# Attention scores as two 64-row tiles in half steps, a new order of the TensorE slot, and one copy that frees a bank

## The reference

```python
# block 1, attention: 16 heads of 16
zn = (z - mu) / sqrt(var + EPS) * ln_scale + ln_bias
q, k, v = heads of zn @ w_qkv
att = softmax(q @ k.T / sqrt(16))            # 1024 x 1024 for each of 4 x 16 heads
block1 = z + (att @ v) @ w_proj + b_proj
# block 2: a gated shared network for all rows, and for 512 routed rows
# one of 8 experts, the two mixed by a softmax of two gate scores
```

## Time and profile before

| | before |
|---|---|
| median of 3 runs | 1079.07 us |
| the profiled execution, its own time | 1083.07 us |
| its span, first to last instruction | 1081.3 us |
| TensorE busy | 981.1 us (91%) |
| VectorE busy | 868.7 us (80%) |
| ScalarE busy | 600.4 us (56%) |
| GpSimd busy | 249.0 us (23%) |
| mean granted TensorE clock | 0.955 |

### The profile page before, as it was taken

One profiled execution on the slowest core, in us unless ns is written; L12 is line 12 of the kernel. 1 busy time (PEld: TensorE's weight loads), 2 busy tenths in 40 slices (PEclk: granted clock), 3 DMA queues, 4 the chain that ended last, 5 costly groups with the idle time before them and its releaser, 6 DMA issues.

```text
span 1081.3 us, 14462 instructions
## 1 busy us (share of the span) xinstructions
PE 981.1 (91%) x5348; PEld 389.9 (36%) x5348; DVE 868.7 (80%) x1762; ACT 600.4 (56%) x699; POOL 249.0 (23%) x297
## 2 busy tenths in 40 slices
PE   4279999999999999999999999999999999829983
PEld 3122332323343344333342343333423432317762
DVE  5288888899988989998889899989899896165655
ACT  3025677677765675667757756677467566600010
POOL 4060001101614220146321312433032024320102
PEclk9597999999999999999999999999999999957996
DMA  9905100510350204111601032016110001410001
GB/s 171 131 1 67 53 25 16 79 41 1 67 92 5 75 12 59 49 40 40 93 26 40 1 44 67 9 40 114 43 40 2 1 1 29 167 59 0 1 1 58
DMA packets 46518, 50.27 MB, mean 46 GB/s; under 512 B 8416, under 2 KB 39408, under 8 KB 46064
## 3 DMA queue, kind: packets, MB, share of 16 engines
q1 hardware_dynamic: 45104, 47.51, 20.9%
q10 hardware_dynamic: 960, 0.79, 0.7%
q0 software_dynamic: 384, 1.05, 0.3%
HBM read 13.94 MB, written 8.91 MB: 21 GB/s over the span
## 4 chain that ended last, share of the span: by engine, by line
PE 72%; DVE 21%; ACT 2%; DMA 2%; issue 2%; POOL 1%; SPq 0%; ACTq 0%; POOLq 0%; DVEq 0%
PE sc L832 20%; PE obank L846 16%; PE ring L818 13%; DVE mx L1052 13%; PE ring L739 9%; PE ring L761 5%; PE sc L922 4%; PE ring L731 3%; DVE st L987 2%; PE ring L872 2%; ACT prob L666 1%; DMA kp<-parts 1%; DVE hid L1009 1%; PE ring L866 1%; DMA x_sb<-x 0%
## 5 line engine op out<-in xcount | busy, mean ns | idle before, releaser
L1052 DVE TENSOR_REDUCE mx<-ring 128x1 f32<-128x512 f32 x1024 | 649.9, 684 | 82.2 <-PE ring L818 74.4
L666 ACT ACTIVATE prob<-sc 128x1024 f32<-128x1024 f32 x512 | 501.0, 1022 | 269.2 <-PE sc L832 269.1
L846 PE MATMUL obank<-prob,vaug 128*32 128x512 f32 x2048 | 273.3, 606 | 0.7 <-ACT prob L666 0.7
L832 PE MATMUL sc<-qp,kp 112*128 112x512 bf16 x1024 | 267.7, 383 | 1.5 <-DMA qp<-mp 0.7
L818 PE MATMUL ring<-kp,qp 48*128 48x512 bf16 x1024 | 224.8, 391 | 34.1 <-issue 20.0
L818 PEld LDWEIGHTS ring<-kp,qp 48*128 48x128 bf16 x1024 | 57.5, 93 | 360.9 <-DVE mx L1052 189.4
L832 PEld LDWEIGHTS sc<-qp,kp 112*128 112x128 bf16 x1024 | 83.8, 98 | 115.4 <-issue 38.7
L501 POOL TENSOR_SCALAR parts<-resid 128x1024 bf16<-128x1024 f32 x14 | 14.7, 1051 | 328.9 <-DVE resid L1042 328.6
L846 PEld LDWEIGHTS obank<-prob,vaug 128*32 128x32 f32 x2048 | 40.3, 108 | 61.9 <-issue 52.4
L731 PE MATMUL ring<-ident,zn 128*128 128x128 f32 x128 | 21.8, 310 | 31.9 <-DVE zn L1003 19.9
L739 PE MATMUL ring<-w,yT 128*128 128x256 f32 x192 | 48.6, 395 | 1.8 <-ACT yT L592 1.8
(11 more groups left out here) (178 smaller groups left out, 785.3 us busy)
## 6 DMA issues: line engine op xcount, KB each, us to landing
kp<-parts SPq DMA_DIRECT2D x96, 128.0 KB, 5.0
qp<-parts SPq DMA_DIRECT2D x180, 64.0 KB, 2.6
x_sb<-x SPq DMA_DIRECT2D x7, 1024.0 KB, 5.9
x_scratch<-x SPq DMA_DIRECT2D x4, 1024.0 KB, 4.4
out<-hid SPq DMA_DIRECT2D x4, 1024.0 KB, 4.6
kp<-ew SPq DMA_DIRECT2D x1, 2048.0 KB, 7.8
x_sb<-x SPq DMA_DIRECT2D x2, 512.0 KB, 4.6
qp<-mp SPq DMA_DIRECT2D x64, 4.0 KB, 1.7
```

The source lines that it names most:

```text
L666: nc.scalar.activation(prob[:, e % 2, 2 * a:2 * a + 2, :].rearrange("p g n -> p (g n)"), sbuf2[a][:, :], ACT.Exp, scale=0.25).then_inc(s_f ...
L832: ins = nc.tensor.matmul(dst[:, j * HALF:(j + 1) * HALF], kp[0:KM, h, kt * P:(kt + 1) * P], qp[0:KM, qh, h, :], start=True, stop=True)
L846: ins = nc.tensor.matmul(obank[i * VW:(i + 1) * VW, :], vaug[:, b % 2, kt, c0:c0 + VW], prob[:, v % 2, i, :], start=(kt == 0), stop=(kt == ...
L1052: nc.vector.tensor_reduce(mx[:, u % 2, n:n + 1], src[:, :], AX.X, ALU.max).then_inc(rv_free, 1)
```

## The change: what it does

In a slot TensorE now does the ring items first, then six pairs of matmuls and the value product. A pair is one matmul on rows 0 to 63 and one on rows 64 to 111. A score buffer is filled in two half steps: the first writes the largest products of both heads (`start=True`), the second adds the small ones (`stop=True`). The second half step waits on a new semaphore `s_largest` until the first is complete. ScalarE does all ring items of a slot before its exponentials. For `qk`, the fp32 copy alone frees the bank, and the bf16 copy is made from it in SBUF after a wait for it. Those who waited for the bf16 copy by `ra_free` now wait on `s_part`.

```diff
@@ ScalarE, ring_item of "qk" and the slot
-                    nc.scalar.activation(qkf[:, half], src[:, :], ACT.Copy).then_inc(s_part, 1)
-                    nc.scalar.activation(parts[:, c % 2, 0, half], src[:, :], ACT.Copy).then_inc(ra_free, 1)
+                    nc.scalar.activation(qkf[:, half], src[:, :], ACT.Copy).then_inc(ra_free, 1)
+                    sc.wait_ge(ra_free, TAKEN[key][1] + 1)
+                    nc.scalar.activation(parts[:, c % 2, 0, half], qkf[:, half], ACT.Copy).then_inc(s_part, 1)
...
-                items = [key for key in RING_AT[t] if key[0] in BY_ACT]
+                for key in RING_AT[t]:
+                    if key[0] in BY_ACT:
+                        ring_item(key)
                 for a in range(2):
...
-                    for key in items:
-                        if (key[0] in ("qk", "v")) == (a == 1):
-                            ring_item(key)
@@ residual, on VectorE (on GpSimd the same)
-                ve.wait_ge(ra_free, TAKEN["qk", b, c, 1][1] + 1)
+                ve.wait_ge(s_part, 2 * n + 2)
@@ TensorE
-                def scores(a):
+                def scores(a, largest):
...
-                    for j in range(2):
-                        h = g * GH + 2 * a + j
-                        ins = nc.tensor.matmul(dst[:, j * HALF:(j + 1) * HALF], kp[0:KM, h, kt * P:(kt + 1) * P],
-                                               qp[0:KM, qh, h, :], start=True, stop=True)
-                    ins.then_inc(s_full, 1)
+                    if largest:
+                        dst = open_s(2 * e + a)
+                    else:
+                        dst = sbuf2[a]
+                        pe.wait_ge(s_largest, 2 * e + a + 1)
+                    for low in range(2):
+                        j = low if largest else 1 - low
+                        h, rows = g * GH + 2 * a + j, slice(64 * low, 64 + KR * low)
+                        ins = nc.tensor.matmul(dst[:, j * HALF:(j + 1) * HALF], kp[rows, h, kt * P:(kt + 1) * P],
+                                               qp[rows, qh, h, :], start=largest, stop=not largest)
+                    ins.then_inc(s_largest if largest else s_full, 1)
...
-                if 0 <= e < NS:
-                    scores(0)
-                    scores(1)
                 for key in RING_AT[t]:
                     if key[0] not in ("max", "mt", "ot"):
                         ring_item(key)
+                if 0 <= e < NS:
+                    scores(0, True)
                 if t < NS:
                     max_products(range(0, 2))
+                if 0 <= e < NS:
+                    scores(1, True)
+                    scores(0, False)
+                    scores(1, False)
+                if t < NS:
+                    max_products(range(2, 4))
                 if 0 <= e - 1 < NS:
                     value_product(e - 1)
-                if t < NS:
-                    max_products(range(2, 4))
```

More of the change, by code:

```diff
@@ L231, in build @@
         s_free = sem("score_buffer_taken")
+        s_largest = sem("largest_products_summed")
         r_full = sem("ring_filled")
@@ L357, in _ @@
                 if part == 0:
-                    sp.wait_ge(ra_free, TAKEN["qk", 0, 0, 1][1] + 1)
+                    sp.wait_ge(s_part, 2)
                 elif part == 1:
@@ L492, in residual @@
                 n = 2 * KD * b + c
-                pool.wait_ge(ra_free, TAKEN["qk", b, c, 1][1] + 1)
+                pool.wait_ge(s_part, 2 * n + 2)
                 pool.wait_ge(s_third, n)
@@ L646, in _ @@
                 if part == 0:
-                    sc.wait_ge(ra_free, TAKEN["qk", 0, 1, 1][1] + 1)
+                    sc.wait_ge(s_part, 4)
                 elif part == 1:
@@ L820, in max_products @@
                                          start=True, stop=True).then_inc(r_full, 1)
-                def scores(a):
+                def scores(a, largest):
                     u, kt = e // 8, e % 8
                     g, qh = u % HU // NH, u % NH
-                    dst = open_s(2 * e + a)
                     if e == 0 and a == 0:
                         pe.wait_ge(s_fixed, 32)
-                    if kt == 0 and a == 0:
+                    if kt == 0 and a == 0 and largest:
                         pe.wait_ge(s_mrow[u % 2], 32 * (u // 2 + 1))
-                    for j in range(2):
-                        h = g * GH + 2 * a + j
-                        ins = nc.tensor.matmul(dst[:, j * HALF:(j + 1) * HALF], kp[0:KM, h, kt * P:(kt + 1) * P],
-                                               qp[0:KM, qh, h, :], start=True, stop=True)
-                    ins.then_inc(s_full, 1)
+                    if largest:
[9 more added lines that the diff above has]
+                    ins.then_inc(s_largest if largest else s_full, 1)
                 def value_product(v):
```

## The result

The changed kernel takes 1112.61 us (median of 4 runs, 1111.58 to 1113.86) against 1079.43 for the kernel before (4 runs beside it): ratio 1.030, 95% interval 1.028 to 1.033. It is slower by 33 us, where 29 were forecast. The profiled execution took 1112.55 us, its span is 1110.7, 29.4 above that of before.

A forecast was written before the change was run, and what follows sets the result against it. The prediction took TensorE to bound the kernel, VectorE 0.2 behind. Slots 27.9, last steps 6.9, absorbed -6 and prologue 0.3 gave +29.1: 1112 profiled, 1108 us on the median (2.7% slower), range 1095 to 1132.

The forecast's parts named there:

- the last steps: Steps after the last max product (e = 244 to 255): from 1.96 to 2.69 each, 6.9 us slower in all.
- TensorE bounds a plain slot, by 0.2 over VectorE: In a slot without a ring item (2.61 us) TensorE never pauses; VectorE's four maxima need 2.40.
- Modes: six pairs, 2.42: TensorE's work in a slot without a ring item: six pairs at 0.22, 0.10 and 1.00, 0.2 less than now.
- The ring's chain: Fourth max product waits for the first one's bank, 1.18 after its start; slots without ring items go from 2.61 to 2.71.
- The exponentials' chain: Buffer 1's next first half step waits for its exponential: 2.69 a step, hidden by 0.02 beside max products.
- Slots with ring items: Each item adds its stream, as before, and one more mode change, 0.10: from +0.03 (`ot`) to +0.19 (`qk`) a slot.
- What absorbs some: Slots already held by other waits, and those just behind them, feel the added wait less: -6 us, bounds 0 and 12.
- The last 4 us: Step from the profiled execution, forecast at 1112, to the median, taken as 4.0 below it: 1108 us.
- ScalarE's edits: `qk` bank freed 0.59 earlier: gain of 0 to 0.5 in the first slots; copies in the prologue +0.3; moved waits nothing.
- the rival at 1133: Pairs cost more than they stream: half steps 0.32 apart, +25, 1133 us; chance 0.15, of which 0.12 near 1120 to 1133.
- The rival on the fast side: The bank wait does not bind: slots without ring items at 2.42 to 2.45, about 1057 us; chance 0.05.

## Why the prediction was right

The direction was right, and so was the mechanism, with one weight misplaced. The size was near, 33 for 29; that the profiled execution came out within 0.3 us of its sum, and the last steps to the 0.1, is luck, as errors met in both.

- *TensorE bounds a plain slot, by 0.2 over VectorE.* Plain slots held 2.61 with shorter maxima. But elsewhere VectorE bounded more than I saw: 37 us went with half of its maxima's columns.
- *Modes: six pairs, 2.42.* 2.44 with both chains cut. The saving of 0.2 a slot is real and was never collected.
- *The ring's chain, 2.71.* M3 1.16 to 1.17 after M0 where I had 1.18, 0.24 (plain) to 0.27 (`qk`) after M2 where I had 0.30, VectorE 0.22 idle where I had 0.3; 2.70 with exponentials cut.
- *The exponentials' chain, 2.69, "hidden by 0.02".* Here lay the error of weight. It is 2.70, a tie with the ring's: cutting either one left plain slots at 2.70. By the half steps in the old order it suffices for the whole loss in plain slots. I presented the ring as the cause and this as a second chain that matters in the last steps; in plain slots it is as much the cause. The last steps cost 6.9, to the 0.1, but not by my reckoning. In the kernel before twelve of them, from value product to value product, took 25.8 us, 2.15 each, and not the 1.96 that I read out of the earlier trace rows: ScalarE wasn't all that held them. They take 31.6 now, +5.8. The other 1.1 belongs to where I count from, as M0 of slot 255 now stands 1.57 ahead of its slot's value product and not 0.32.
- *Slots with ring items.* Measured from the traces as medians, M0 to M0, each distance put down to the item of the second slot or the `mt` or `ot` of the first: `qk` +0.29 where I had +0.19; `z`, `a`, `x` +0.21 against +0.15; `p`, `h` +0.22 and `w` +0.19 against +0.11; `mt` +0.07 against +0.08; `ot` +0.07 against +0.03. The term that failed is the item's stream, which I took over from the kernel before, where the item stands behind scores in the same mode. Behind a change of mode its first pass costs more. A `qk` item takes 1.92 from its start to the next L0 behind the value product (18 times, with 0.53 from its first pass to its second and 0.43 between the others). Behind an `mt`, which is in full mode like the item, it takes 1.81 in the same kernel (6 times), as it did behind whole scores before:

```profile
371.92 0.28 PE L877 MATMUL ring<-ident,nm 128*16 128x128 f32 x1
372.03 1.88 PE L762 MATMUL ring<-zT,wk 128*128 128x512 f32 x4
373.85 0.39 PE L840 MATMUL sc<-qp,kp 64*128 64x512 bf16 x2
```

In the kernel with half steps alone it stands behind the half steps and takes 1.92 as well, so it is the change of mode and not the value product. That its weights are then no longer loaded behind a running matmul is argued from this, not shown.
- *What absorbs some, -6.* The sum from M0 of slot 12 to that of slot 255 came out at 27.9, my sum without this term, where with it I had 21.9. But the differences of medians, kind by kind and times the counts, add up to 33.4: the slots were undercounted by 5.5, most of it in those with items, and 5.5 was absorbed. So the 6 stands, and it is the items' term that was too small. The 2.6 before slot 12 and the 2.7 after the last value product no term had.
- *The last 4 us.* For the profiled execution I had +29.1, to 1112; it took 1112.55, its span +29.4 (27.9 + 6.9 - 2.6 - 2.7). Slots and last steps cost 34.8 where I had 28.8, and the 5.3 that came off outside them hid this. The median came out 4.6 above my 1108, since I had taken the profiled execution's 4.0 above the median along, while that of the changed kernel stands on its median. The lower clock of before's profiled execution behind the last value product, told above, fits that, and so does the medians' difference of 33.2, near the 34.8.
- *ScalarE's edits, nothing.* 1.0004. I had M2 as "late by some 0.2 with both copies"; it was late by 0.12 and covered.
- *The rivals.* Pairs stand 0.22 apart, so the rival at 1133 falls. The Trainium skill (TensorE: Matmul & The Clock Gate, Part 3: Packing small matmuls) gives 3.07 for four row tiles, from which I had estimated 0.28 a pair; with two tiles, here, no such loss is to be seen (three pairs in 0.67). The rival on the fast side needed both chains broken, and the kernels with work left out bear that out: 1026.8 with both cut, 1075.2 with max products first and the exponentials cut.

## What to carry to other kernels

Splitting one accumulation in two half steps lengthens the time for which a buffer is held before its reader can start (from the first scores to the exponential 0.70 before and 1.18 now, in the plain slots shown), and if the steps of two buffers alternate, it couples buffers that were independent: count the chain reader, first half step, other buffer's second half step, reader, before counting matmuls. Price every reuse of a bank from both ends of its reader's latency, and do it for each chain by itself: here two chains tied at 2.70, and an experiment on either one alone would have cleared it. And a saving in a stage that is bound by 0.2 is worth nothing if it moves the two uses of a bank 0.4 closer.

## What the runs showed of the hardware

- A full-mode fp32 item of four 512-column passes takes 1.92 behind a value product in 32-column mode or behind 64-row half steps, and 1.81 behind full-mode work. The difference is in the first pass, 0.53 in place of 0.43.
- Pairs of matmuls on rows 0 to 63 and 64 to 111 can follow one another at 0.22 each, the distance of two single full-mode matmuls before, whether they open an accumulation, close it, or write another bank.
- ScalarE's bf16 copy of 512 columns takes 0.63 out of SBUF in the changed kernel and 0.59 out of PSUM, so moving its source costs 0.04.
